# Two mixture-of-experts layers: the first expert projections contract 192 rows as 128 + 64 instead of 96 + 96

## The reference

```python
# layer 0: 8 experts, F = 768
mid = relu(einsum('bsd,fd->bsf', x, W1[e]) + b1[e])
ye  = einsum('bsf,df->bsd', mid, W2[e]) + b2[e]
out = out + w[..., e:e+1] * ye            # w: softmax of the two best scores, else 0
# layer 1: 16 experts, F = 512
h = silu(einsum('td,eid->tei', xf, w1)) * einsum('td,eid->tei', xf, w3)
y = einsum('tei,edi->td', h * comb[:, :, None], w2)
```

## Time and profile before

| | us |
|---|---|
| median of 3 runs | 1753.22 (1749.12 to 1757.63) |
| the profiled execution | 1757.27 |
| its span | 1755.6 |
| first expert layer, 716 to 927 | 211 |
| second expert layer, 1434 to 1683 | 249 |

### The profile page before, as it was taken

How to read it: one execution, slowest core, us unless ns; L and a number is a source line. 1 busy time by engine, 2 the same in 40 slices (tenths; PEclk the granted TensorE clock), 3 DMA queues, 4 the chain that set the end, 5 groups by cost and what they waited for, 6 DMA issues and landing times.

```text
span 1755.6 us, 23414 instructions
## 1 busy us (share of the span) xinstructions
PE 1325.4 (75%) x7336; PEld 911.9 (52%) x7336; DVE 819.8 (47%) x1551; ACT 495.5 (28%) x834; POOL 494.0 (28%) x394
## 2 busy tenths in 40 slices
PE   0666687788768673988894678998998879999960
PEld 0212132332322362888884464665657469999950
DVE  2488975876688853111111635345463412222212
ACT  0445346446535210233231212415151101101100
POOL 4756644544544451000003400000000600000025
PEclk9868678889878875799997658898888889999985
DMA  4200000000000014888883100000000368888843
GB/s 118 43 1 0 1 1 1 1 1 1 1 1 1 1 55 144 240 256 250 241 263 89 48 1 0 1 0 0 0 1 3 108 178 242 245 242 239 245 129 94
DMA packets 56062, 152.96 MB, mean 87 GB/s; under 512 B 9632, under 2 KB 30880, under 8 KB 51200
## 3 DMA queue, kind: packets, MB, share of 16 engines
q1 hardware_dynamic: 44096, 127.80, 26.1%
q0 software_dynamic: 11904, 24.40, 4.6%
HBM read 133.09 MB, written 19.07 MB: 87 GB/s over the span
## 4 chain that ended last, share of the span: by engine, by line
PE 48%; DVE 16%; DMA 12%; issue 9%; POOL 5%; ACT 3%; DVEq 3%; POOLq 2%; SPq 1%; ACTq 1%; PEldq 0%
PE ps L720 35%; DMA expert<-arena 8%; DVE arena L1432 5%; PE ps L848 3%; PE ps L1090 3%; POOL arena L484 2%; DMA arena<-sorted 2%; DVE ps L1427 2%; PE ps L873 1%; PE ps L1082 1%; PE ps L986 1%; DVEq L1428 1%; ACT arena L587 1%; DVE st L1188 1%; POOL h_rows L350 1%
## 5 line engine op out<-in xcount | busy, mean ns | idle before, releaser
L720 PE MATMUL ps<-arena 96*128 96x128 f32 (+1 forms) x1680 | 224.1, 290 | 8.3 <-issue 8.3
L1432 DVE TENSOR_TENSOR_SCAN arena<-arena,ps 128x1024 f32<-128x1024 f32 x96 | 219.5, 2287 | 13.4
L720 PEld LDWEIGHTS ps<-arena 96*128 96x128 f32 (+1 forms) x1680 | 215.2, 192 | 12.4 <-issue 12.1
L720 PE MATMUL ps<-xTF,wreg 96*128 96x512 f32 x352 | 203.4, 725 | 9.0 <-DVE arena L1593 4.8
L848 PE MATMUL ps<-arena,pick 32*128 32x512 f32 x384 | 133.4, 778 | 95.9 <-DVE arena L1432 92.9
L472 POOL DMA_DIRECT2D expert<-arena x88 | 47.9, 544 | 508.5 <-DVE arena L1555 225.7
L385 POOL DMA_INDIRECT sorted<-x_rows,row_i x64 | 62.6, 979 | 414.1 <-DVEq L1337 395.3
L587 ACT ACTIVATE arena<-ps,wreg 128x508 f32<-128x508 f32 x192 | 120.9, 681 | 200.4 <-PE ps L860 199.6
L720 PE MATMUL ps<-arena,ew_in 96*128 96x128 f32 x1248 | 154.6, 284 | 7.7 <-issue 7.7
L720 PE MATMUL ps<-xT,wreg 96*128 96x512 f32 (+3 forms) x296 | 133.9, 599 | 29.7 <-ACT arena L548 15.6
L720 PEld LDWEIGHTS ps<-arena,ew_in 96*128 96x128 f32 x1248 | 150.2, 199 | 11.5 <-issue 11.4
(11 more groups left out here) (203 smaller groups left out, 1799.8 us busy)
## 6 DMA issues: line engine op xcount, KB each, us to landing
ew_in<-in_e_in SPq DMA_DIRECT2D x24, 768.0 KB, 6.3
arena<-in_e_in SPq DMA_DIRECT2D x24, 768.0 KB, 6.8
ew_out<-in_e_out SPq DMA_DIRECT2D x20, 675.0 KB, 5.5
arena<-in_e_out SPq DMA_DIRECT2D x20, 675.0 KB, 5.4
ew_in<-in_e_in SPq DMA_DIRECT2D x20, 576.0 KB, 5.1
arena<-in_e_in SPq DMA_DIRECT2D x20, 576.0 KB, 5.0
ew_out<-in_e_out SPq DMA_DIRECT2D x24, 384.0 KB, 6.6
arena<-in_e_out SPq DMA_DIRECT2D x24, 384.0 KB, 7.2
```

Of the source, the lines that this page charges most:

```text
L720: last = pe.matmul(o, lhs, rhs, start=(n == 0), stop=(n == len(pairs) - 1))
L1432: ve.tensor_tensor_scan(hid[k % 3], dec[k % 3], bx.rearrange("p x t -> p (x t)"), 0.0, ALU.mult, ALU.add)\
```

## The change

The 192 features are split as 128 + 64. `xbT[k]` now has the first 128 features on 128 partitions, and the last 64 features twice: on partitions 0 to 63 and again on 64 to 127. The weights lie on 128 partitions: the first 128 rows of every tile, and then, for two tiles that belong together, the 64 remaining rows of the one on partitions 0 to 63 and of the other on 64 to 127. For each two tiles the kernel issues two matmuls over 128 rows and then two matmuls over 64 rows in the two halves of the array, into two different PSUM banks. `turn` gets three operations per block: a transpose of 128 columns, one of 64 columns, and a matmul by the identity that writes the second copy of the 64 features to partitions 64 to 127. Bytes per weight load are the same (1152 words on 128 partitions instead of 1536 on 96 in layer 0, 1536 instead of 2048 in layer 1). VectorE's copy at L1533 covers 128 partitions, ScalarE reads the six tiles of layer 0 from alternating banks, and the offsets of the buffers follow.

```diff
-        xbT = [part(6656 + 256 * k, 2 * P, KH).rearrange(...) for k in range(2)]
+        xbT = [part(6656 + 256 * k, 2 * P).rearrange(...) for k in range(2)]
...
-            expert_loads(0, E0, NB0, e0_in, e0_out, 2 * EF0 * P, EF0 * D + EF0 + D)
-            expert_loads(1, E1, NB1, e1_in, e1_out, 4 * EF1 * P, EF1 * D)
+            expert_loads(0, E0, NB0, e0_in, e0_out, 3 * EF0 * P // 2, EF0 * D + EF0 + D)
+            expert_loads(1, E1, NB1, e1_in, e1_out, 3 * EF1 * P, EF1 * D)
...
-                        act.activation(hbT[k][:, f, :], ps[:, 1 + 2 * k + f // 4, (f % 4) * P:(f % 4 + 1) * P], ACT.Relu,
+                        act.activation(hbT[k][:, f, :], ps[:, 1 + 2 * k + f % 2, (f // 2) * P:(f // 2 + 1) * P], ACT.Relu,
...
                         pe.wait_ge(s_xb[m][k], i * 32 + h * 16 + 16)
-                        for c in range(2):
-                            last = pe.transpose(ps[0:KH, 7 * k, c * P:(c + 1) * P], xb[k][:, c * KH:(c + 1) * KH], ident)
-                        last.then_inc(s_bt[m], 1)
+                        pe.transpose(ps[:, 7 * k, 0:P], xb[k][:, 0:P], ident)
+                        pe.transpose(ps[0:64, 7 * k, P:2 * P], xb[k][:, P:D], ident)
+                        pe.matmul(ps[64:P, 7 * k, P:2 * P], xb[k][:, P:D], ident, start=True, stop=True).then_inc(s_bt[m], 1)
...
-                        for half in range(2 if gated else 1):
-                            for f in range(fg):
-                                bank = 1 + 2 * k + (half if gated else f // 4)
-                                base = 2 * n_in * half
-                                last = accumulate(ps[:, bank, (f % 4) * P:(f % 4 + 1) * P],
-                                                  [(e_in[m][j][:, base + c * n_in + f * P:base + c * n_in + (f + 1) * P], xbT[k][:, c, :])
-                                                   for c in range(2)])
+                        w, x = e_in[m][j], xbT[k]
+                        for p in range(fg if gated else fg // 2):
+                            outs, firsts = [], []
+                            for half in range(2):
+                                outs.append(ps[:, 1 + 2 * k + half, p * P:(p + 1) * P])
+                                f = half * fg + p if gated else 2 * p + half
+                                firsts.append(w[:, f * P:(f + 1) * P])
+                            at_b = ((2 if gated else 1) * fg + p) * P
+                            for half in range(2):
+                                pe.matmul(outs[half], firsts[half], x[:, 0, :], start=True, stop=False)
+                            for half in range(2):
+                                r = slice(64 * half, 64 * half + 64)
+                                last = pe.matmul(outs[half], w[r, at_b:at_b + P], x[r, 1, :], start=False, stop=True)
                         last.then_inc(s_bh[m], 1)
                         pe.drain().then_inc(s_w1f[j], 1)
...
-                        ve.tensor_copy(xbT[k], ps[0:KH, 7 * k, 0:2 * P].rearrange("p (c t) -> p c t", c=2))\
+                        ve.tensor_copy(xbT[k], ps[:, 7 * k, 0:2 * P].rearrange("p (c t) -> p c t", c=2))\
```

More of the change, by code:

```diff
@@ L152, in tower @@
         EW = 11264
-        e_in = [[w[0:KH, :] for w in ew_in_all] + [part(EW + step * x, n, KH) for x in range(2)]
-                for step, n in ((2886, 1536), (2816, 2048))]
+        e_in = [[w[:, :] for w in ew_in_all] + [part(EW + step * x, n) for x in range(2)]
+                for step, n in ((2502, 1152), (2304, 1536))]
         e_out = [[w[:, :] for w in ew_out] + [part(EW + step * x + n, step - n) for x in range(2)]
-                 for step, n in ((2886, 1536), (2816, 2048))]
+                 for step, n in ((2502, 1152), (2304, 1536))]
         QUADS = (0, NB0 // 4)
         xb = [part(6144 + 256 * k, D) for k in range(2)]
-        xbT = [part(6656 + 256 * k, 2 * P, KH).rearrange("p (k t) -> p k t", k=2) for k in range(2)]
+        xbT = [part(6656 + 256 * k, 2 * P).rearrange("p (k t) -> p k t", k=2) for k in range(2)]
         hbT = [part(7168 + 768 * k, EF0 * P).rearrange("p (f t) -> p f t", f=EF0) for k in range(2)]
@@ L977, in expert_blocks @@
                         pe.sem_inc(s_w2f[j], 1)
-                n_in = fg * P
                 at = QUADS[m] * 16
@@ L1751, with rest @@
                            a["L0_attn_A_log"].reshape(DG, 4, 4, 8, NST).transpose(4, 3, 0, 2, 1).reshape(P, -1)], 1)
-    e0_in = np.stack([halves(w.T).reshape(KH, -1) for w in a["L0_ffn_W1"]])
+    def rest(w):
+        return w[P:].reshape(D - P, -1, 2, P).transpose(2, 0, 1, 3).reshape(P, -1)
+    e0_in = np.stack([np.concatenate([w.T[:P], rest(w.T)], 1) for w in a["L0_ffn_W1"]])
     e0_out = np.stack([np.concatenate([groups(w2.T).reshape(P, -1), columns(b1, P), np.broadcast_to(b2, (P, D))], 1)
                        for w2, b1, b2 in zip(a["L0_ffn_W2"], a["L0_ffn_b1"], a["L0_ffn_b2"])])
-    e1_in = np.stack([np.concatenate([halves(w1.T).reshape(KH, -1), halves(w3.T).reshape(KH, -1)], 1)
+    e1_in = np.stack([np.concatenate([w1.T[:P], w3.T[:P], np.concatenate([w1.T[P:], w3.T[P:]])], 1)
                       for w1, w3 in zip(a["L1_ffn_w1"], a["L1_ffn_w3"])])
```

## The result

The changed kernel takes 1834.7 us, median of 4 runs (1827.9 to 1835.9), against 1753.8 us for the kernel before on the same chip: a ratio of 1.045 (95% interval 1.0405 to 1.0496), 80.9 us slower. The forecast was 1821 us, with a range of 1790 to 1862.

The account below looks back on a forecast made before the run. PE was taken to bound the second layer, stores one at a time the first. Plus 50, 16 and 2 us (second layer, first layer, starts) on 1757.3 gave 1825; less 4 to the median, 1821 us, range 1790 to 1862.

Parts of the forecast that it names:

- The price of a change of shape: In the first projections, each switch between 128-row and 64-row matmuls was to cost 0.194 us.
- Rival (a): Shape changes between 128 and 64 rows are free: 1734 us, or no change with slow stores; chance 0.08.
- Couples side by side: In the first projections, two 64-row matmuls run together, starting within 0.01 us of each other.
- part 1: In the first projections, two tiles take 6 slots instead of 8: minus 0.224 us, plus 0.007 us of lag.
- The turn: At each block's turn, the added matmul and its shape changes cost 0.562 us, 1.12 us per pair.
- The steady pairs: A pair of blocks takes 13.3 to 13.4 us in the second expert layer, about 12.5 in the first.
- The first layer passes from the stores to PE: PE's first-layer pair grows by 1.76 to 12.52 us, passing the stores' 11.71 by 0.81; waits for tokens go.
- The clock: In the second layer the granted clock stays at 1.00; under 0.95 the prediction would be wrong.
- rival (c): PE's clock falls to 1.2 GHz; for a third of the second layer plus 48 us, 1869; chance 0.07.
- the term for the starts at 1.2 GHz: Blocks running at 1.2 GHz at the start of each expert layer add 2 us.
- Loads over 128 partitions at no cost: Expert weight loads carry the same bytes in 128 pieces instead of 96, adding nothing to the time.
- The stores' floor of 10.5 us: Two second-layer stores, one after the other, need 10.5 us: 4.3 us landing and 0.95 us to next issue.

Follow-up runs that it names:

- `one_change`: Changed kernel with all 128-row matmuls of a block issued first, then all 64-row couples; ratio 0.989 to the kernel before, 1730.6 us.
- `turn_three`: Changed kernel with a turn of three transposes, one of features 64 to 191, and no matmul by the identity; ratio 1.022 to the kernel before.
- `stores_inc_before`: Kernel before with GpSimd issuing the next store before waiting for the last, buffers freed by a semaphore increment instead of a drain; ratio 0.9918.
- `padded_loads`: Kernel before with first weights padded by zeros from 96 to 128 rows, PE still reading 96; ratio 0.9929 to the kernel before, 1739.0 us.
- `full_rows`: Changed kernel with each tile's second matmul over all 128 rows, so no 64-row groups and a different result; ratio 1.0188 to the kernel before.
- `two_turns`: Changed kernel with 128-row matmuls first, couples after, and a turn of two transposes, weights packed to fit; ratio 0.9621 to the kernel before, 1688 us.
- `control`: The kernel before itself, run and traced once more without any change; ratio 1.0007, 1752.6 us.
- `more_changes`: Changed kernel with each tile's 64-row part directly after its 128-row matmul, a change of shape after every two passes; ratio 1.2748 to the kernel before.

## Why the prediction was right, point by point

- **The price of a change of shape** was taken as 0.194 us from 128-column loads beside 32-row groups. Measured for 64 rows: 0.193, with loads starting 0.09 us behind the end of the stream, as said. The cycle of two tiles follows: 0.892 + 0.388 - 0.217 = 1.063 worked out, 1.06 seen. Rival (a) falls. The Trainium skill, page "TensorEngine Tiling (Array Packing)", section "Key Properties", says that changing the tiling mode drains the engine; this case's trace now agrees for 64-row groups too, with 0.09 us of emptying at each change.
- **Couples side by side**: held (`one_change`, eight slots for sixteen passes). The saving of part 1 is real; it is smaller than the price of the two changes between which it stood, 0.217 against 0.386. Grouped, with one change a block inside it, it shows as a gain: 10.94 us a second-layer pair against 11.23, in spite of the dearer turn.
- **The turn** was put at +1.12 us a pair and measured 0.98 in the turn plus 0.10 in the bare load behind it, 1.08. `turn_three` takes 0.85 of it away again, by three transposes in one shape.
- **The steady pairs**: 13.33 forecast, 13.30 measured, in the second layer; 12.52 and 12.48 in the first. Against the mean pairs of before (11.30, 11.71) that is 2.00 and 0.77, where 2.10 and 0.81 were forecast.
- **The first layer passes from the stores to PE**: held. Its chain has no store, the waits for tokens are gone. That PE alone needs 10.76 in the kernel before is what `stores_inc_before` (10.75) and `padded_loads` (10.74) show, each taking away the stores' hold in its own way.
- **The clock**: 1.00 in both layers' steady parts, as said; over the whole second layer, its start included, 0.96, just above the 0.95 that was to count as rival (c). But the term for the starts at 1.2 GHz was mis-sized: 2 us forecast, some 9 to 10 measured. In the second layer the second and third pair took 17.02 and 15.57 us, 6.0 above two steady ones; in the kernel before 10.08 and 11.89, 0.6 below. In the first they are 13.26 and 15.86, 4.2 above; before 1.3. The granted clock goes with it. The first two rows are the kernel before at this place in its second layer, the third is `one_change`, the last `full_rows`:

```profile
1417.00:1434.00 17.00, 10.10 (x70) 9.24 (x68) 1.53 (x3) 1.10 (x2) 0.00 (x0) 0.70 1.01 254
1434.00:1450.00 16.00, 14.98 (x116) 14.48 (x115) 4.97 (x11) 1.29 (x3) 1.18 (x2) 1.00 0.83 224
1434.00:1451.00 17.00, 15.97 (x147) 14.24 (x146) 2.96 (x7) 1.79 (x3) 1.18 (x2) 1.00 0.76 264
1433.00:1446.00 13.00, 12.38 (x92) 10.98 (x92) 3.19 (x7) 1.59 (x3) 0.59 (x1) 1.00 0.58 206
```

  The kernel before is at 1.00 from 1434 on, its stage having begun at 1417; the changed one, which begins it at about 1441, is at 0.50 to 1462 and at a mean of 0.82 from there to 1479, though PE has work 15.61 of 16 us. `one_change` and `full_rows`, which begin this layer at 1415 and 1417, are granted 1.00 from 1434 and 1433 on, and `full_rows` needs 11.35 and 12.32 us for the second and third pair. It has the loads and the turn of the changed kernel and lacks only the 64-row groups. So frequent changes of shape in the first projections put off the rise of the clock, rival (c) in small; by what way, no run here tells.
- **Loads over 128 partitions at no cost**: wrong in the kernel's favour. They are a gain of 0.7% (0.3 to 1.1) by themselves where stores bind (`padded_loads`), and invisible in the changed kernel, which PE bounds throughout.
- **The stores' floor of 10.5 us** in rival (a) was wrong for the same reason: it took 4.3 us of landing as fixed. With first weights on 128 partitions the stores of `two_turns` land in 3.5 us, two of them with 0.95 each between need 8.9, and a pair of 9.83 goes through. By these numbers a free change of shape would have gained more than the 19 us of rival (a).

The sum: 24 and 20 pairs were to add 50 and 16 us, and the starts 2. Measured in the layers are 51.3 and 17.1, with 1.6 behind them: 70 for 68. That this comes out within 2 us is partly luck: the starts cost 7 to 8 us more than forecast, and against that stand steady pairs that grew a little less (about 3 us over both layers) and the first stretch of each layer, from its first turn to its second, which took 5.4 and 5.2 us instead of 6.9 and 6.9. The remaining 7 us of the profiled spans lie in stages with the same instructions; `control` shows such differences without any change. The last 4 us, up to the medians' 80.9, are how far the profiled execution of the kernel before stood above its median; that of the changed kernel did not.

## What to carry to other kernels

Packing small contractions side by side pays only if the matmuls of one array shape are grouped: here a change of shape costs 0.19 us, nearly two passes of 128 columns, so one change inside a block gains, and seven (five in the first layer) lose. Before a second copy of an operand is made by a column group, look for a split (features 0 to 127 and 64 to 191) whose plain transposes leave it on the right partitions. And a load's partitions are part of its price: time a transfer that others queue behind on 128 partitions before taking it as given.

## What the runs showed of the hardware that was not expected

- **Loads over 96 partitions hold the DMA engines longer than their bytes.** Single 8192-byte pieces of the second layer's first weights took 505 ns in the mean in the kernel before and 350 ns in `padded_loads`. What is loaded beside them slows too: the 3072-byte pieces of the same layer's second weights, on 128 partitions in both, took 166 and 122. In the first layer this is less clear: the 5400-byte pieces took 279 and 217, but in `one_change`, where all weights lie on 128 partitions, 281. The Trainium skill, page "SBUF — State Buffer", section "Door 1: The DMA port swizzle", makes bandwidth depend on how many of 16 ports the partitions reach; by its mapping 96 partitions reach all 16, half of them with half the partitions, so that by the count of ports alone nothing would be lost. The runs show a loss; an estimate from that mapping for the fuller ports, two thirds of the bytes instead of half, would be 1.33 times the time, where the pieces show 505/350 = 1.44. Whether the uneven ports are the cause no run here tells.
- **A drain on GpSimd waits for a store that was just issued**: 0.13 us with none in flight, 6.05 with one, ending with that store's landing, and the increment in its place took the loss away.
- **With frequent changes of shape the granted clock is lower**: 0.72 to 0.75 in `more_changes` with PE 97% occupied, and at the start of the second layer 0.50 from 1446 to 1462 in the changed kernel, where `full_rows` had 1.00 within 17 us of the layer's begin.
